# Behind the last attention head of a fused two-layer transformer kernel: experts' bias in three parts by single-pass products, outputs in front of row sums, idle multiplies on TensorE

## What is computed

```python
out = softmax(q @ k.T * scale) @ v              # 8 heads
x = x + out @ Wo + bo
xf = layernorm(x)
scores = softmax(xf @ gw + gb)                  # 32 experts in 8 groups of 4
# groups are ranked by the sum of their two best scores; 4 groups stay;
# the 4 best experts of these have their scores as weights, cw (tokens x 32)
y = sum over e of cw[:, e] * ((silu(xf @ w1[e] + b1[e]) * (xf @ w3[e] + b3[e])) @ w2[e] + b2[e])
z = (silu(xf @ sw1 + sb1) * (xf @ sw3 + sb3)) @ sw2 + sb2
x = x + y + z
```

## Time and profile before

| | |
|---|---|
| median of three runs | 1462.4 us (1462.14 to 1464.22) |
| the profiled execution | 1464.5 us, of which 1462.7 are the span from first to last instruction |
| TensorE busy, share of the span | 95% |
| VectorE, GpSimd, ScalarE busy | 75%, 64%, 54% |
| mean granted TensorE clock | 0.954 of full |
| the part that the change touches | from about 1340 us to the end |
| the pairs of experts, without a pause of TensorE | 1377.9 to about 1456 us |

### The profile page before, as it was taken

The page is one execution under the profiler, slowest core; times in us unless marked ns, Lnnn a source line. Parts: engine busy times, 40 slices in busy tenths (PEclk is TensorE's granted clock), DMA queues, the critical chain, the costliest instruction groups (busy, mean ns, idle before and its releaser), DMA issues.

```text
span 1462.7 us, 19933 instructions
## 1 busy us (share of the span) xinstructions
PE 1391.6 (95%) x6191; PEld 793.8 (54%) x6191; DVE 1095.5 (75%) x1484; ACT 793.9 (54%) x1576; POOL 941.2 (64%) x542
## 2 busy tenths in 40 slices
PE   5999998887999999999999999999999999998898
PEld 3877775533455555555554555455555555554565
DVE  8976666388888788778868878887887886666555
ACT  3458886321556556556655655555555555553332
POOL 5001113231889888978988897898898899886110
PEclk8999999655999999999999999999999999998799
DMA  6630000310000200100020020002002000000011
GB/s 173 206 126 18 18 17 7 71 22 2 0 1 1 49 1 1 33 17 1 1 49 1 1 46 4 1 1 49 1 0 47 1 1 1 1 1 13 18 38 40
DMA packets 77372, 39.45 MB, mean 27 GB/s; under 512 B 62047, under 2 KB 70000, under 8 KB 77002
## 3 DMA queue, kind: packets, MB, share of 16 engines
q1 hardware_dynamic: 77290, 38.36, 10.5%
HBM read 24.66 MB, written 13.68 MB: 26 GB/s over the span
## 4 chain that ended last, share of the span: by engine, by line
PE 86%; DVE 8%; DMA 3%; ACT 2%; issue 1%; POOL 0%; SPq 0%; ACTq 0%; DVEq 0%; POOLq 0%
PE ps L1384 24%; PE ps L1371 14%; PE ps L1372 12%; PE ps L1337 9%; DVE chunk_max L943 3%; DMA v_scratch<-v_stage 3%; PE ps L1324 3%; PE ps L1528 2%; PE ps L1199 2%; PE ps L1197 2%; PE ps L1208 2%; PE ps L1198 2%; PE ps L1209 2%; PE ps L1210 2%; PE ps L1316 1%
## 5 line engine op out<-in xcount | busy, mean ns | idle before, releaser
L524 POOL TENSOR_TENSOR psums<-psums,probs 126x1024 f32<-126x1024 f32 (+1 forms) x392 | 821.2, 2095 | 122.6 <-ACT probs L705 75.7
L705 ACT ACTIVATE probs<-ps 126x512 f32<-126x512 f32 (+1 forms) x816 | 416.2, 619 | 273.2 <-PE ps L1372 272.3
L943 DVE TENSOR_REDUCE chunk_max<-ps 128x2 f32<-128x1008 f32 (+1 forms) x416 | 472.7, 1181 | 77.1 <-PE ps L1337 75.7
L1384 PE MATMUL ps<-probs,v_mem 126*64 126x512 f32 (+1 forms) x1632 | 389.7, 598 | 0.0
L1371 PE MATMUL ps<-q_heads,ring 128*126 128x512 f32 (+1 forms) x816 | 342.9, 420 | 1.1
L1372 PE MATMUL ps<-q_low,ring 128*126 128x512 f32 (+1 forms) x816 | 322.5, 395 | 0.0
L994 DVE TENSOR_TENSOR xn<-xn,probs 126x512 f32<-126x512 f32 x126 | 231.1, 1834 | 29.9 <-ACT probs L705 25.6
L671 ACT CAST ring<-ps 64x252 fp32r<-64x252 f32 (+1 forms) x356 | 128.1, 360 | 136.3 <-PE ps L1324 133.2
L1384 PEld LDWEIGHTS ps<-probs,v_mem 126*64 126x64 f32 (+1 forms) x1632 | 111.5, 136 | 165.5 <-issue 120.9
L1371 PEld LDWEIGHTS ps<-q_heads,ring 128*126 128x126 f32 (+1 forms) x816 | 152.0, 186 | 88.6 <-issue 44.5
L1337 PE MATMUL ps<-ring,q_heads 64*128 64x504 f32 (+1 forms) x416 | 171.9, 482 | 18.1 <-DVE chunk_max L943 9.7
(11 more groups left out here) (200 smaller groups left out, 1412.8 us busy)
## 6 DMA issues: line engine op xcount, KB each, us to landing
v_scratch<-v_stage SPq DMA_DIRECT2D x51, 252.0 KB
v_mem<-v_scratch SPq DMA_DIRECT2D x8, 1606.5 KB
ctx_mem<-in_ctx_t SPq DMA_DIRECT2D x3, 803.2 KB, 8.9
vslot<-in_ctx_rows SPq DMA_DIRECT2D x51, 47.2 KB
pair_w<-in_f_pairs SPq DMA_DIRECT2D x17, 128.0 KB, 2.1
pair_w<-in_f_pairs SPq DMA_DIRECT2D x17, 65.0 KB, 1.8
x_tok<-in_x SPq DMA_DIRECT2D x1, 512.0 KB, 4.1
wo<-in_c_wo SPq DMA_DIRECT2D x1, 512.0 KB
```

Source lines behind the costliest of these rows:

```text
L524: pool.tensor_tensor(sums[0:r, 0:width], sums[0:r, 0:width], probs[0:r, n % PROBS, 0:width], ALU.add).then_inc(c_sum, 1)
L705: act.activation(probs[0:r, n % PROBS, cols(half)], ps[0:r, score_bank(t, half), :], ACT.Exp, scale=float(HD) ** -0.5).then_inc(c_exped, 1)
L943: dve.tensor_reduce(chunk_max[:, h % 2, i:i + 2, c], ps[:, banks[0]:banks[1] + 1, 0:group_tiles(c) * KT], AX, ALU.max).then_inc(c_reduced, 1)
L1384: ins = pe.matmul(ps[half * HD:(half + 1) * HD, B_ACC, :], v_tiles[0:r, h % 2, t, :], probs[0:r, n % PROBS, cols(half)], start=(t == 0), s ...
```

## The change

- The experts' bias becomes an `fp32r` product over 96 rows: `b2_parts` has the rounded `b2` in rows 0 to 31 and 32 to 63, written by ACT, and the remainder in rows 64 to 95, written by POOL. `cw_parts` gets the rounded weights once more in rows 64 to 95, copied by ACT instead of `cw_t`. The zeros that `gate` needs move from `cw_parts` to `spread1`, rows 64 to 95, and are still set by POOL. `gate(0, 0)` waits for the third part too.
- In the last head `project_out` comes before `sum_rows`, whose result goes to bank 0 instead of `B_AUX`, and it no longer waits for the reciprocal.
- `warm(n, bank, width)` multiplies `ident` by a piece of `wo1` into a bank that nobody reads, in plain float32: 11 times with 256 columns behind the row sums, once with 64 columns behind each of the eight transposes of `xn`, once with 256 behind these, once before the first `up`, 10 times behind it, and twice before the wait for `cw`.
- The semaphore `f_mask` is merged into `f_step`; `cw_t` leaves the memory of the context.

```diff
--- before.py
+++ after.py
@@ -47,6 +47,7 @@
 PAIRS = ((3, 4), (5, 6))
 B_MAX = 3
 B_AUX, B_ACC = 5, 7
+B_LAST_SUMS = 0
 FIRST_PAIRS, FIRST_KP = ((0, 1), (2, 3), (6, 7)), 4
 
 
@@ -208,8 +209,8 @@
         a_cslot, a_vproj, a_vevac, a_vout = (sems(f"a_{n}", CH) for n in ("cslot", "vproj", "vevac", "vout"))
 
 
-        f_pe, f_step, f_mask, f_w, f_biassb, f_gelu, f_masktsb, f_masked, f_x = (
-            sem(f"f_{n}") for n in ("pe", "step", "mask", "w", "biassb", "gelu", "masktsb", "masked", "x"))
+        f_pe, f_step, f_w, f_biassb, f_gelu, f_masktsb, f_masked, f_x = (
+            sem(f"f_{n}") for n in ("pe", "step", "w", "biassb", "gelu", "masktsb", "masked", "x"))
         PE_BIAS, PE_LOGITS, PE_HIDDEN, PE_MASK, PE_SPREAD, PE_OUT = 1, 2, (3, 4, 6, 7), 5, 8, 12
         q_zero, ring_rows = sem("q_zero"), sem("ring_rows")
 
@@ -227,6 +228,7 @@
 
         g_step, g_logits, g_exp, g_cw, g_cwt, g_cwtsb, g_spread_ready, g_store = (
             sem(f"g_{n}") for n in ("step", "logits", "exp", "cw", "cwt", "cwtsb", "spread_ready", "store"))
+        g_b2 = sem("g_b2")
         g_xs, g_whi, g_wlo = sem("g_xs"), sem("g_whi"), sem("g_wlo")
         g_w13 = sems("g_w13", 2)
         g_w, g_u, g_silu, g_h, g_gate, g_hg, g_y, g_fin = (
@@ -254,7 +256,6 @@
         gl, gp, cw = over_ctx(TT, E1), over_ctx(TT, E1), over_ctx(TT, E1)
         gm, gs = over_ctx(TT), over_ctx(TT)
         pmax, pmin, qmax, qmin, keep = (over_ctx(TT, GROUPS) for _ in range(5))
-        cw_t = over_ctx(TOK)[0:E1, :]
         x3_t = over_ctx(TOK)
         pair_w = sb("pair_w", [P, 2, PAIR_W])
 
@@ -319,6 +320,7 @@
             parts = sb_c("parts", [P, 2 * TOK + 8 * P], F32R)
             cw_parts = sb_c("cw_parts", [3 * E1, TOK], F32R)
             spread1 = sb_c("spread1", [3 * E1, G1, P], F32R)
+            b2_parts = sb_c("b2_parts", [3 * E1, D], F32R)
             silu = sb_c("silu", [P, 2, HALF])
             hgate = sb_c("hgate", [P, 2, HALF])
             spread_raw = sb_c("spread_raw", [3 * E1, G1, P], BF16)
@@ -536,8 +538,11 @@
 
             pool.wait_ge(c_attended, TILES * HEADS)
             pool.wait_ge(c_sum, adds_to(HEADS - 1, TILES - 1))
-            pool.memset(f32(cw_parts[2 * E1:3 * E1, :]), 0.0).then_inc(g_xs, 1)
-            pool.wait_ge(g_xs, 2)
+            pool.memset(f32(spread1[2 * E1:3 * E1, :, :]), 0.0).then_inc(g_b2, 1)
+            pool.wait_ge(g_b2, 2)
+            pool.tensor_tensor(b2_parts[2 * E1:3 * E1, :], b2_1[:, :], f32(b2_parts[0:E1, :]), ALU.subtract).then_inc(g_b2, 1)
+            pool.wait_ge(g_b2, 3)
+            pool.wait_ge(g_xs, 1)
             pool.tensor_tensor(x_lo, xn_t[:, :], f32(x_hi), ALU.subtract).then_inc(g_xs, 1)
             with pool.Fori(0, G1 // 2) as i:
                 for s in range(2):
@@ -730,13 +735,16 @@
                     act.wait_ge(g_u[1], last_up)
                 act.copy(w_parts[:, s, 0, :], pair_w[:, s, 0:2 * P]).then_inc(g_whi, 1)
 
+            act.wait_ge(in_f1, 16 * 5)
+            for part in range(2):
+                ins = act.copy(b2_parts[part * E1:(part + 1) * E1, :], b2_1[:, :])
+            ins.then_inc(g_b2, 1)
             act.wait_ge(tr_act, 4)
             act.wait_ge(tr_dve, 4)
             act.copy(x_hi, xn_t[:, :]).then_inc(g_xs, 1)
             for s in range(2):
                 w_hi(s, 16, None)
-            act.wait_ge(in_f1, 16 * 5)
-            act.copy(spread1[:, :, :], spread_raw[:, :, :])
+            act.copy(spread1[0:2 * E1, :, :], spread_raw[0:2 * E1, :, :])
             act.wait_ge(g_exp, 1)
             act.activation(gp, gp, ACT.Exp).then_inc(g_exp, 1)
             turned(4, x3_t)
@@ -755,8 +763,8 @@
             w_hi(0, 32, 1)
             act.wait_ge(g_cwt, 1)
             act.copy(halves(cw_parts[0:E1, :]), ps[0:E1, 1:4:2, :]).then_inc(g_cwtsb, 1)
-            act.wait_ge(g_spread_ready, 1)
-            act.copy(halves(cw_t), ps[0:E1, 1:4:2, :]).then_inc(g_cwtsb, 1)
+            act.wait_ge(g_cwtsb, 1)
+            act.copy(cw_parts[2 * E1:3 * E1, :], f32(cw_parts[0:E1, :])).then_inc(g_cwtsb, 1)
 
             def act_pairs(i, last):
                 m = [act.snap(2 * i + n) for n in (1, 2, 3)]
@@ -901,7 +909,7 @@
             dve.wait_ge(f_step, 4)
             for t in range(TT):
                 ins = dve.tensor_scalar(mask0[:, t, :], iota[:, 0:E0], idxf8[:, t, 0:1], None, ALU.is_equal)
-            ins.then_inc(f_mask, 1)
+            ins.then_inc(f_step, 1)
             for n in range(2 * G0):
                 g, half = n // 2, n % 2
                 dve.wait_ge(f_gelu, n + 1)
@@ -960,7 +968,8 @@
                 dve.wait_ge(c_sums, h + 1)
                 if h:
                     dve.wait_ge(c_x, 2 * h)
-                dve.reciprocal(rden[:, :], ps[:, B_AUX, 0:TT]).then_inc(c_rden, 1)
+                bank = B_LAST_SUMS if h == HEADS - 1 else B_AUX
+                dve.reciprocal(rden[:, :], ps[:, bank, 0:TT]).then_inc(c_rden, 1)
 
             def add_output(h, part, banks):
                 dve.wait_ge(c_out, 2 * h + part + 1)
@@ -1276,7 +1285,7 @@
                 hidden(n)
             for g in range(EARLY[0], EARLY[1]):
                 k_proj(g)
-            pe.wait_ge(f_mask, 1)
+            pe.wait_ge(f_step, 5)
             for t in range(TT):
                 ins = pe.transpose(ps[0:E0, B_MASK[t // 4], tile_cols(t % 4)], mask0[:, t, :], ident[:, :])
             ins.then_inc(f_pe, 1)
@@ -1393,13 +1402,15 @@
                     rows = psums[:, h % 2, tile_cols(t)]
                     if h == HEADS - 1 and t >= TT // 2:
                         rows = psums_v[:, h % 2, tile_cols(t - TT // 2)]
-                    ins = pe.matmul(ps[:, B_AUX, t:t + 1], rows, ones[0:KT, 0:1], start=True, stop=True)
+                    bank = B_LAST_SUMS if h == HEADS - 1 else B_AUX
+                    ins = pe.matmul(ps[:, bank, t:t + 1], rows, ones[0:KT, 0:1], start=True, stop=True)
                 ins.then_inc(c_sums, 1)
 
             def project_out(h, part, banks):
                 if part == 0:
                     pe.wait_ge(c_acc, h + 1)
-                    pe.wait_ge(c_rden, h + 1)
+                    if h < HEADS - 1:
+                        pe.wait_ge(c_rden, h + 1)
 
                 for u in (2 * part, 2 * part + 1):
                     for half in range(2):
@@ -1489,12 +1500,24 @@
                             pe.wait_ge(c_exped, 2 * (TILES * h + block_tiles(b)[-1] + 1))
                             k_proj_parts(g, B_KEYS)
             pe.wait_ge(c_x, 2 * HEADS - 2)
-            sum_rows(HEADS - 1)
             for part in range(2):
                 project_out(HEADS - 1, part, PAIRS[part])
-
-
-            turn(3, xn, 3)
+            sum_rows(HEADS - 1)
+
+            def warm(n, bank, width=2 * D):
+
+                for _ in range(n):
+                    pe.matmul(ps[:, bank, 0:width], ident[:, :], wo1.rearrange("p h d -> p (h d)")[:, 0:width],
+                              start=True, stop=True)
+
+            warm(11, 1)
+            for t in range(TT):
+                pe.wait_ge(ln_out, 3 * TT + t + 1)
+                ins = pe.transpose(ps[:, 6 + t // 4, tile_cols(t % 4)], xn[:, t, :], ident[:, :])
+                if t % 4 == 3:
+                    ins.then_inc(tr_psum, 1)
+                warm(1, 1, HD)
+            warm(1, 1)
             turned(3)
             pe.wait_ge(in_f1, 16 * 5)
             for t in range(TT):
@@ -1530,22 +1553,27 @@
 
 
             pe.wait_ge(g_step, 1)
-            pe.wait_ge(g_xs, 3)
+            pe.wait_ge(g_xs, 2)
+            warm(1, 5)
             for half in range(2):
                 up(0, 0, half, 1, shared=True)
+            warm(10, 5)
             turned(4)
             for half in range(2):
                 down(0, half, g_h, 1, start=True)
             up(1, 1, 0, 2)
+            warm(2, 5)
             pe.wait_ge(g_cw, 1)
             for t in range(TT):
                 ins = pe.transpose(ps[0:E1, 1 + 2 * (t // 4), tile_cols(t % 4)], cw[:, t, :], ident[:, :])
             ins.then_inc(g_cwt, 1)
             pe.wait_ge(g_spread_ready, 1)
+            pe.wait_ge(g_cwtsb, 2)
             gate(0, 0)
-            pe.wait_ge(g_cwtsb, 2)
+            pe.wait_ge(g_b2, 3)
             for half in range(2):
-                pe.matmul(ps[:, 6 + half, :], b2_1[:, :], cw_t[:, cols(half)], start=False, stop=False, skip_group_check=True)
+                pe.matmul(ps[:, 6 + half, :], b2_parts[:, :], cw_parts[:, cols(half)], start=False, stop=False,
+                          skip_group_check=True)
 
             def two_pairs(i, last):
                 m1, m2, m3 = 2 * i + 1, 2 * i + 2, 2 * i + 3
```

## The result

The changed kernel takes 1457.2 us, the median of seven executions (1451.1 to 1459.4), against 1462.6 for the kernel before in the same comparison: a ratio of 0.9959 with a 95% interval of 0.9944 to 0.9974, 5.4 us less. The profiled execution took 1457.2 (span 1455.4).

A forecast was written before the change was run, and what follows sets the result against it. TensorE, 86% of the last-ending chain, was taken as the bound: 1.75 + 3.3 + 2.35 - 1.7 = 5.7 us off the profiled 1464.5. Less 0.8 for profiled-versus-timed differences, 4.9 below the median: 1457.5, range 1455.0 to 1461.8.

The forecast's parts named there:

- Outputs in front: Last head: outputs before row sums let the adds, and so the norm, start 0.4 us earlier.
- Idle multiplies in their waits: Norm and router: eleven multiplies take 4.7 us at full clock inside the norm's wait; 0.36 per transposed tile.
- Logits: Router: sixteen logit instructions take 1.9 us at full clock instead of 3.59 at half clock.
- Down products: First experts: the four down products take 1.7 us instead of 3.53.
- Bias: Experts' bias at the gate: two single-pass products instead of four instructions gain 3.3 us, 2.7 if cold.
- Clock behind the bias: Start of the pairs: 2.35 us of cold penalty go, but a new 3.4 us cold stretch costs 1.7.
- rival B: Clock holds everywhere, through the wait for the router's weights too: 7.4 us gained, 1455.0; chance 15%.
- Rival A: Clock falls during the norm's transposes, narrow fillers being too light: 2.6 us gained, about 1459.8; chance 28%.
- Rival C: Idle multiplies run at 1.2 GHz throughout, not counting as work: 15.5 us lost, 2.7 gained, 1475; chance 5%.

The follow-up runs named there:

- no_fill: The changed kernel without any idle multiplies, new order and single-pass bias kept: 1456.3 us, ratio to before 0.9953.
- only_bias: The kernel before with the single-pass bias alone, old order and no idle multiplies: 1456.3 us, ratio to before 0.9957.
- old_order_2: Second run of the changed kernel with row sums, reciprocal and outputs in the old order: 1456.8 us, ratio to before 0.9965.
- no_narrow: The changed kernel without the eight 64-column multiplies between the transposes of the norm's tiles: 1457.8 us, ratio to before 0.9974.
- old_bias: The changed kernel with the experts' bias as before (plain float32 over 32 rows), order and multiplies kept: 1460.2 us, ratio to before 0.9986.
- gap_trim: The changed kernel with five multiplies in the wait for the weights' parts, nine instead of ten and one instead of two elsewhere: 1455.7 us, again 1454.5.
- old_order: First run of the changed kernel with row sums, reciprocal and outputs in the old order: 1456.7 us, ratio to before 0.9963.
- rows32: The changed kernel with all idle multiplies over 32 rows instead of 128, same columns: 1472.8 us, ratio to before 1.0075.

## Why the prediction held, and where its reasons did not

The time was forecast at 1457.5 and came out at 1457.2; the tail gained 5.6 where the sum said 5.7. That both are so close is partly luck: the bias gained less than its term and the clock more, and of the 0.8 taken off for the difference between the profiled and the timed executions, for which there was no row, the times show 0.2 at most (5.4 against 5.6). Step by step, as distances behind the last addition:

- *Outputs in front.* Adds start at 2.8 instead of 3.2: the 0.4 forecast. Right; that it also lets the wide multiplies begin ahead of the clock's fall was not in the forecast.
- *Idle multiplies in their waits.* The clock held, the eleven took 5.0 and ended before the first tile. Right. A narrow one was mis-sized: 0.17 for its two instructions and not 0.24, a tile 0.29 and not 0.36, so the last transpose, and with it ScalarE's queue, is 0.3 earlier, where I had put 0. The one-column sums were the wrong row to take the price from. That made VectorE's gain 1.1 instead of 0.85 (reduction and gated product), but the ten multiplies ended 0.3 behind the gated product's first half and the two 0.15 behind the weights, and ate the surplus: the gate gained 1.73, as forecast (1.75).
- *Logits* 1.94: right (1.9). *Down products* 1.72 in the chain: right.
- *Bias.* Pairs 1.3 to 1.5 behind the gate instead of 4.0, 2.5 to 2.7 gained rather than 3.3, as the cold stretch began in the middle of the gate product: the forecast had the cold case at 2.7 and put the warm one into its sum. ScalarE's two small copies took 0.60 together and its third part 1.04 beside VectorE's 1.22, both hidden as said.
- *Clock behind the bias.* One cold stretch of 3.4 us, as forecast in length. It begins in the gate product, so that only 2.2 us of it lie in the pairs and cost them 1.1, not 1.7; the rest is in the bias's term.

What failed is the attribution. The sum gave 1.75 to the gate's move and took 1.7 for a cold stretch, as two independent terms, and it laid the second to the wait for the weights' parts, which every kernel without multiplies in it has. `no_fill` and `only_bias` have the same transposes and the same wait of 2.3 us, and no cold stretch behind them; nor have `old_order_2` and `no_narrow`, with multiplies. What goes with the fall is when the wait ends. Where the gate stands at 30.4 or 30.5 us behind the heads and nothing fills the wait (the changed kernel twice, `old_bias`), the clock falls within 0.4 us; where it stands at 31.6 to 32.2 (the four just named) and the bias is single-pass, it stays high. So the multiplies bring the cold stretch by what they win: an early gate. Of the 1.45 won there 0.5 go to gate and bias products at half clock, and the 2.2 us of pairs that are cold give back 1.1. The bias alone carries 5.4 of the 5.6 measured, and the order 0.3. I had noted that the clock would have to be held through the gap to gain more (rival B, 7.4, tail 113.5): `gap_trim` reaches that in the tail, 7.2, with a few multiplies that the change doesn't have.

Rival A's fall happens when the narrow multiplies are missing, but its sum of 2.6 was wrong twice. It put the gate 1.4 us later than before, where `no_narrow` has it 0.6 earlier (31.6 against 32.2), and it let the pairs be cold behind it (1.6), which they were not. Rival C was priced at 12.6 above before; made to happen it was 10 above in the time and 7.7 in the tail. Eleven multiplies cost 8.9 (9.7 forecast) and a tile 1.0 rather than 0.7, but the first expert products brought the clock back 30.6 us behind the heads, so the ten took 4.6 and not 8.8: the gate came 11.5 late and not 15.5.

The Trainium skill, "TensorE: Matmul & The Clock Gate", section "Part 4: PE-mode transpose", says that transposes do not count as busy in the same way as other products. The trace of `no_narrow` agrees as far as it goes: with the narrow multiplies out, 1.0 us of wait and 2.0 us of transposes lie in front of the fall at 10.3, and with them in the clock held.

What stays open: why a wait that ends at 30.4 is followed by a fall and one that ends at 31.6 or later is not. What TensorE does in front of the gate, 1.0 us of transposes and 2.3 of wait, is the same in both; `old_order` (gate at 33.4, fall 1.2 us behind it) and `rows32` (43.7, 0.5 us) show that a later gate is not safe either, and no run moved the wait alone. And whether the 1.6 us of `gap_trim` reach the time in every execution.

## What to carry to other kernels

Before a stretch is filled with idle work to hold TensorE's clock, remove the slow step next to it, and then try each without the other: here one 4-byte product over 32 rows, made into single-pass products, was worth 5.4 us, and thirty-three multiplies around it nothing on top. Don't add up a gain from a held clock ahead and a cold stretch behind as independent terms: here the same wait, moved 1.5 us ahead by the first, brought the second, and only with that wait filled too did the gain show in the tail. Where runs scatter by 2 us, compare profiles from a fixed event (here the last addition) to the end, and take more than one profile before an edit that hangs on the clock is priced.

## What the runs showed of the hardware

TensorE busy without a gap was not TensorE at full clock. 26 us of multiplies over 32 rows, transposes, 32-column products and, at the end, the first expert products, 100% busy, ran at 1.2 GHz throughout (`rows32`), while the same multiplies over 128 rows held it. In `old_bias` the clock, at 0.50 since 30.8, was still there when the four 32-row bias instructions had run for 3.8 us, and came back at 41.0, after some 6 us of the pairs; in the changed kernel, with two 96-row ones, it was back at 34.1. At half clock the one-column row sums slow down too: 3.2 us instead of 1.9 for sixteen, and their weight loads fill that time (1.42 and 1.83 us for eight each in `old_order`). And one kernel fell to the low clock at different places in two executions (0.5 and 3.5 us behind the heads in the two runs of the old order), with 2.8 us between their tails.
